# The last mixture-of-experts layer: 32 steps of 256 rows of one expert and four steps of 128-row tiles of any expert, in place of 39 steps of 256 rows

## The reference, cut to what matters

```python
def _L1_ffn_ref(x, Wr, br, W1, b1, W2, b2):
    K = 2
    E = Wr.shape[-1]                                   # 8 experts, W1 256 x 1024, W2 1024 x 256
    scores = jnp.einsum('bsd,de->bse', x, Wr) + br
    _, topk_idx = jax.lax.top_k(scores, K)
    indicator = jax.nn.one_hot(topk_idx, E, dtype=scores.dtype).sum(-2)
    weights = jax.nn.softmax(jnp.where(indicator > 0, scores, -jnp.inf), axis=-1)
    out = jnp.zeros_like(x)
    for i in range(E):
        xi = x * indicator[..., i:i + 1]
        h = jax.nn.relu(jnp.einsum('bsd,dh->bsh', xi, W1[i]) + b1[i])
        yi = jnp.einsum('bsh,hd->bsd', h, W2[i]) + b2[i]
        out = out + yi * weights[..., i:i + 1]
    return out
...
x = x + _L1_ffn_ref(_layernorm(x), L1_ffn_Wr, L1_ffn_br, L1_ffn_W1, L1_ffn_b1, L1_ffn_W2, L1_ffn_b2)
```

## Time and profile before

| | us |
|---|---|
| median of 3 runs | 1501.83 (1501.78 to 1501.98) |
| span of the profiled execution, first to last instruction | 1499.1 |
| of it `experts`, from the first row load (1050.4) to the end | 448.7 |
| PE busy over the span | 1272.8 (85%) |
| DVE / ACT / POOL busy over the span | 1052.8 / 821.5 / 523.5 |

### The profile page before, as it was taken

The page is one execution under the profiler, slowest core; times in us unless marked ns, Lnnn a source line. Parts: engine busy times, 40 slices in busy tenths (PEclk is TensorE's granted clock), DMA queues, the critical chain, the costliest instruction groups (busy, mean ns, idle before and its releaser), DMA issues. The chain is left out here.

```text
span 1499.1 us, 29224 instructions
## 1 busy us (share of the span) xinstructions
PE 1272.8 (85%) x8841; PEld 970.2 (65%) x8842; DVE 1052.8 (70%) x2033; ACT 821.5 (55%) x1209; POOL 523.5 (35%) x429
## 2 busy tenths in 40 slices
PE   8789999959975748998899998651899999999996
PEld 4456766744432647865567667650789989899995
DVE  5769999785699784557688887775456565656653
ACT  4565655465699677426778776650344343434431
POOL 2066676500000000000767675476023333332333
PEclk9899999979998558959999999555899999999998
DMA  6100000000134753001132232465222222222220
GB/s 216 60 8 1 0 0 0 1 1 0 43 147 163 262 205 122 1 1 45 31 123 75 87 123 70 142 211 178 69 47 51 42 49 46 42 46 44 50 40 10
DMA packets 63789, 106.87 MB, mean 71 GB/s; under 512 B 9776, under 2 KB 50832, under 8 KB 63088
## 3 DMA queue, kind: packets, MB, share of 16 engines
q1 hardware_dynamic: 49424, 89.17, 18.0%
q0 software_dynamic: 14304, 16.93, 6.2%
HBM read 67.89 MB, written 40.01 MB: 72 GB/s over the span
## 5 line engine op out<-in xcount | busy, mean ns | idle before, releaser
L2120 POOL DMA_INDIRECT out<-ex_yo,ex_mt x78 | 134.2, 1721 | 317.3 <-DVE ex_yo L2095 181.1
L2039 ACT ACTIVATE ex_hT<-ex_ps_h,e_b1T,e_unscale 128x256 f32<-128x256 f32 x312 | 150.8, 564 | 115.2 <-PE ex_ps_h L1997 115.2
L1997 PE MATMUL ex_ps_h<-ex_xT_hi,a_arena 128*128 128x256 f16 x1248 | 212.5, 274 | 0.0
L704 PE MATMUL at_ps_y<-c_VW,at_pT_hi 128*128 (+1 forms) x1024 | 172.8, 274 | 1.3 <-DVE main_x_res L835 1.3
L682 PE MATMUL at_ps_s<-a_arena,at_xnT_hi 128*128 (+1 forms) x512 | 158.6, 393 | 15.9 <-issue 13.1
L1997 PE MATMUL ex_ps_h<-ex_xT_lo,a_arena 128*128 128x256 f16 x624 | 171.0, 274 | 0.0
L2010 PE MATMUL ex_ps_y<-a_arena,ex_hT_lo 128*128 x624 | 170.1, 273 | 0.0
L2010 PE MATMUL ex_ps_y<-e_w_lo,ex_hT_hi 128*128 x624 | 170.1, 273 | 0.0
L2010 PE MATMUL ex_ps_y<-a_arena,ex_hT_hi 128*128 x624 | 170.1, 273 | 0.0
L959 POOL TENSOR_TENSOR at_sc<-at_sc,at_ri 128x960 f32<-128x960 f32 (+1 forms) x96 | 131.9, 1389 | 86.0 <-DVE at_ri L830 85.6
L1201 PE MATMUL gm_bank<-f_xq,f_wide 128*128 (+1 forms) x576 | 128.3, 383 | 20.7 <-ACT gm_stg L1239 16.2
(11 more groups left out here) (323 smaller groups left out, 2805.3 us busy)
## 6 DMA issues: line engine op xcount, KB each, us to landing
at_half<-in_L_ffn_W SPq DMA_DIRECT2D x32, 512.0 KB, 3.9
up_scratch<-gm_stg SPq DMA_DIRECT2D x16, 768.0 KB, 3.2
gm_stg<-up_scratch SPq DMA_DIRECT2D x16, 768.0 KB, 4.4
ex_row<-xs SPq DMA_DIRECT2D x39, 260.0 KB, 2.7
rt_stage<-in_L_ffn_W SPq DMA_DIRECT2D x16, 512.0 KB, 4.8
main_x_res<-in_x SPq DMA_DIRECT2D x8, 512.0 KB, 12.0
out<-main_x_res SPq DMA_DIRECT2D x8, 512.0 KB, 4.1
xs<-rt_pad SPq DMA_DIRECT2D x18, 130.0 KB, 2.1
```

Of the source, the lines that this page charges most:

```text
L704: last = nc.tensor.matmul(ps_y[:, 0:D], a[j][:, n, :], b[:, bass.ds(off + n * D, D)], start=(n == 0 and i == 0), stop=(n == NP - 1 and i = ...
L1997: last = nc.tensor.matmul(ps_h[:, n, :], a[:, bass.ds(e * WN + d * HID + n * P, P)], b[:, d, :], start=(m == 0), stop=(m == 3 * DT - 1))
L2039: last = nc.scalar.activation(hT[:, n, :], ps_h[:, n, :], ACT.Relu, bias=b1T[:, bass.ds(e * HT + n, 1)], scale=unscale[:, 0, bass.ds(e, 1)])
L2120: nc.gpsimd.indirect_dma_start(out=acc[:, :], out_offset=bass.IndirectOffsetOnAxis(ap=mt[j][:, q, 1:2].bitcast(U32), axis=0), in_=yo[j][:, ...
```

## The change

The steps become 36: 32 (`ND`) of 256 rows of one expert as before, and then four (`NM`) that take 128-row tiles, each tile of any expert, two to a step: seven tiles (`NH`), so three steps have two and the last has one. 32 groups of 256 and seven tiles of 128 are always enough for eight experts.

`table` has a place and an expert for 32 + 7 entries. Its computation on DVE shares out the steps of 256: first each expert's full groups of 256, then, while there are any to spare, experts with a rest of more than 128 rows, then those with a smaller rest; what is left becomes 128-row tiles. It has 31 DVE instructions behind the counts where there were 12. POOL sets two constants more (`CONSTS` 12).

In `experts`, every function asks `runs(i)` for the pieces of step i: one piece of 256 for i < 32, and one or two of 128 for the rest. For each piece of a mixed step SP looks up the place and issues a DMA; PE, ACT and DVE look up the expert's number once per piece; `up` and `relu` do each output tile once per piece, on 128 columns; `down` takes each half's expert; `weigh` and `keep_meta` have one instruction per piece where they use the expert's number. `rows_of` and `columns_of` cut the last step's work to its one tile. The loop now covers steps 4 to 27, and 28 to 35 are straight code.

```diff
-NTL = (2 * T + E * (TR - 1)) // TR
+ND = 2 * T // TR
+NH = 7
+NM = -(-NH // 2)
+NTL = ND + NM
...
-        CONSTS = 10
+        CONSTS = 12
...
-            g.iota(tid[:, :], pattern=[[1, NTL]], base=0, channel_multiplier=0,
+            g.iota(tid[:, 0:ND], pattern=[[1, ND]], base=0, channel_multiplier=0,
                    allow_small_or_imprecise_dtypes=True).then_inc(cst, 1)
+            g.iota(tid[:, ND:ND + NH], pattern=[[1, NH]], base=0, channel_multiplier=0,
+                   allow_small_or_imprecise_dtypes=True).then_inc(cst, 1)
+            g.memset(whole[:, E:E + 1], 0.0).then_inc(cst, 1)
...
+        def mixed(i):
+            return isinstance(i, int) and i >= ND
+
+        def runs(i):
+            if not mixed(i):
+                return [(i, 0, Q)]
+            return [(ND + 2 * (i - ND) + q, q, q + 1) for q in range(min(Q, NH - 2 * (i - ND)))]
...
-            for k in range(-lead, 4 + odd):
+            for k in range(-lead, 4):
                 step(k, k % 2)
-            with eng.Fori(2, NTL // 2 - 2, 1) as i:
+            with eng.Fori(2, (ND - 4) // 2, 1) as i:
                 for j in range(2):
-                    step(2 * i + (j + odd), (j + odd) % 2)
-            for k in range(NTL - 4, NTL + lag):
+                    step(2 * i + j, j)
+            for k in range(ND - 4, NTL + lag):
                 step(k, k % 2)
...
             def up(i, j):
-                e = look_up(nc.tensor, 1, i, E - 1)
+                spans = [(look_up(nc.tensor, 1, n, E - 1), slice(q0 * P, q1 * P)) for n, q0, q1 in runs(i)]
...
                     for n in range(4 * g, 4 * g + 4):
-                        m = 0
-                        for d in range(DT):
-                            for a, b in ((whi, xT_hi[j]), (whi, xT_lo[j]), (wlo, xT_hi[j])):
-                                last = nc.tensor.matmul(ps_h[:, n, :], a[:, bass.ds(e * WN + d * HID + n * P, P)], b[:, d, :],
-                                                        start=(m == 0), stop=(m == 3 * DT - 1))
-                                m += 1
+                        for e, at in spans:
+                            m = 0
+                            for d in range(DT):
+                                for a, b in ((whi, xT_hi[j]), (whi, xT_lo[j]), (wlo, xT_hi[j])):
+                                    last = nc.tensor.matmul(ps_h[:, n, at], a[:, bass.ds(e * WN + d * HID + n * P, P)], b[:, d, at],
+                                                            start=(m == 0), stop=(m == 3 * DT - 1))
+                                    m += 1
...
             def down(i, j):
-                e = look_up(nc.tensor, 1, i, E - 1)
+                spans = [(look_up(nc.tensor, 1, n, E - 1), range(q0, q1)) for n, q0, q1 in runs(i)]
...
-                for q in range(Q):
+                for e, q in ((e, q) for e, qs in spans for q in qs):
...
-                    for n in range(4 * g, 4 * g + 4):
-                        last = nc.scalar.activation(hT[:, n, :], ps_h[:, n, :], ACT.Relu,
+                    for n, (e, at) in ((n, span) for n in range(4 * g, 4 * g + 4) for span in spans):
+                        last = nc.scalar.activation(hT[:, n, at], ps_h[:, n, at], ACT.Relu,
                                                     bias=b1T[:, bass.ds(e * HT + n, 1)], scale=unscale[:, 0, bass.ds(e, 1)])
...
-                for q in range(Q):
+                for q in range(rows_of(i).stop):
                     need(pool, added, 16 * (Q * i + q))
                     pool.sem_inc(begun, 1)
...
-            pool.wait_ge(added, 16 * Q * NTL)
+            pool.wait_ge(added, 16 * (Q * ND + NH))
```

More of the change, by code:

```diff
@@ L1611, in route @@
         pad = s.sb("pad", [P, ROW])
[L1612 to L1616, removed]
+        ntf, nti, jump = s.sb("ntf", [P, 2, E]), s.sb("nti", [P, 2, E], I32), s.sb("jump", [P, 2, E])
+        cum, want, give, left = (s.sb(n, [P, 2, E]) for n in ("cum", "want", "give", "left"))
+        whole, lone, spare, twice = s.sb("whole", [P, E + 1]), s.sb("lone", [P, E]), s.sb("spare", [P, 1]), s.sb("twice", [P, 1])
+        tid = s.sb("tid", [P, ND + NH])
+        ge = s.sb("ge", [P, ND + NH, E])
+        tf = s.sb("tf", [P, 2, ND + NH])
         cnt = s.sb("cnt", [P, E], I32)
@@ L1902, in _ @@
             dve.sem_inc(cnt_r, 1)
[L1903 to L1909, removed]
@@ new lines, in _ @@
+            then(v.scalar_tensor_tensor(out=give[:, :, :], in0=cum[:, :, :], scalar=spare[:, 0:1], in1=want[:, :, :],
+                                        op0=ALU.is_le, op1=ALU.mult))
+            v.tensor_tensor(left[:, :, :], want[:, :, :], give[:, :, :], ALU.subtract)
+            then(v.tensor_tensor(lone[:, :], give[:, 0, :], give[:, 1, :], ALU.add))
+            v.tensor_tensor(whole[:, 0:E], ntf[:, 0, :], lone[:, :], ALU.add)
+            then(v.scalar_tensor_tensor(out=left[:, 0, :], in0=left[:, 0, :], scalar=2.0, in1=left[:, 1, :],
+                                        op0=ALU.mult, op1=ALU.add))
@@ new lines, in _ @@
+            v.tensor_tensor_scan(cum[:, 0, :], ones[:, 0:E], whole[:, 0:E], 0.0, ALU.mult, ALU.add)
+            v.tensor_scalar(jump[:, 0, :], whole[:, 0:E], -1.0, float(CAP // TR), ALU.mult, ALU.add)
+            v.tensor_tensor(lone[:, :], whole[:, 1:E + 1], whole[:, 0:E], ALU.subtract)
+            v.tensor_scalar(twice[:, :], whole[:, 0:1], 2.0, None, ALU.mult)
+            then(v.tensor_tensor_scan(cum[:, 1, :], ones[:, 0:E], left[:, 0, :], 0.0, ALU.mult, ALU.add))
+            v.scalar_tensor_tensor(out=jump[:, 1, :], in0=lone[:, :], scalar=2.0, in1=left[:, 0, :],
+                                   op0=ALU.mult, op1=ALU.subtract)
@@ new lines, in _ @@
+            for k, at in enumerate((slice(0, ND), slice(ND, ND + NH))):
+                last = v.tensor_tensor(ge[:, at, :], tid[:, at].unsqueeze(2).to_broadcast([P, (ND, NH)[k], E]),
+                                       per_tile(cum[:, k, :], k), ALU.is_ge)
+            then(last)
+            v.tensor_reduce(tf[:, 1, :], ge[:, :, :], AX.X, ALU.add)
+            then(v.tensor_scalar(jump[:, 1, :], jump[:, 1, :], float(CAP // P), None, ALU.add))
+            for k, at in enumerate((slice(0, ND), slice(ND, ND + NH))):
+                last = v.tensor_tensor(ge[:, at, :], ge[:, at, :], per_tile(jump[:, k, :], k), ALU.mult)
@@ L1917, in _ @@
+            v.tensor_scalar(table[:, 0, ND:ND + NH], tf[:, 0, ND:ND + NH], twice[:, 0:1], float(E * CAP // P), ALU.add, ALU.min)
             lows(highs_to(NK - 1), highs_to(NK))
@@ L1961, in load @@
             def load(i, j):
-                r = look_up(nc.sync, 0, i, E * CAP // TR)
+                rows = TR if not mixed(i) else P
                 need(sp, t_r, i - 1)
                 need(sp, meta_r, i - 1)
-                sp.dma_start(row[j][:, :, :], xs[bass.ds(r * TR, TR), :].rearrange("(q p) d -> p q d", p=P)
-                             ).then_inc(row_in[j], 16)
+                for n, q0, q1 in runs(i):
+                    r = look_up(nc.sync, 0, n, E * CAP // rows)
+                    sp.dma_start(row[j][:, q0:q1, :], xs[bass.ds(r * rows, rows), :].rearrange("(q p) d -> p q d", p=P)
+                                 ).then_inc(row_in[j], 16)
             def step(k, j):
```

83 lines of the change are left out of this document (56 added, 27 removed).

## The result

The changed kernel's median is 1480.45 us where the kernel before has 1501.8, a ratio of 0.9869 with a 95% interval of 0.9824 to 0.9914: faster by 21.3 us, and 1.5 us above the forecast of 1479. The execution that left the profile took 1477.83 us with a span of 1476.0; that of the kernel before took 1500.83 with 1499.1. So the two profiled executions are 23.0 us apart, where the sum had 22.8.

What follows compares the result with a forecast made beforehand. PE was taken to bound `experts`, its sequencer's addresses the mixed `up`. PE's 19.8 plus tail 3.3 less constants 0.3 gave 22.8 us saved: 1501.8 - 22.8 = 1479.0 us, range 1474 to 1485, at chance 0.70.

Steps and rivals of the forecast that it cites:

- mixed `up` of 32, 33, 34, 35: PE's `up` in the four mixed steps, paced by the sequencer's addresses: 7.95, 7.95, 8.6 and 4.1, sum 28.6 us.
- bare look-ups: Sequencer look-ups before the `down` of steps 31 to 34 leave PE idle: 0.9 once, 1.55 three times, 5.55 us.
- PE's balance: On PE, 71.2 us of removed work less the added `down`, transposes, mixed `up` and look-ups: 19.8 us saved.
- tail: After the last `down` but one, three additions on POOL instead of four: 16.6 against 19.95, 3.3 us saved.
- The pace of addresses: PE's sequencer in a mixed `up`: one address per 0.13 us, so 64 need 8.3 us and end last.
- B: Rival: the sequencer isn't the limit; a mixed `up` takes 5.2 us, nothing is bare, time 1463; chance 0.05.
- The lead: PE's sequencer runs 1.1 us ahead before `up`; a second look-up takes 0.65, leaving 0.45 us.
- Rival A: Weight loads pace small matmuls at 0.109 us; a mixed `up` takes 10.5, look-ups are hidden, time 1481.5; chance 0.14.
- Rival C: Clock falls for moments at bare look-ups: 1.7 us each, one to three of them, 1481 to 1484; chance 0.08.
- D: Rival: clock stays at 0.50 through all mixed steps; four `down` cost 21 us more, time 1507; chance 0.03.
- What was to be hidden: Per mixed step of about 15 us, ACT's at most 9.0 and DVE's 9 to 10 stay covered by PE.
- The table: In `route`, 19 more DVE instructions, 5.5 us, stay covered before the first row load; up to 5.5 if not.

Runs made afterwards that it cites:

- early2: The changed kernel with PE looking up all seven tiles' experts behind the `up` of steps 29 to 31, for mixed `up` and `down`; 1470.90 us.
- static_up: The changed kernel with fixed experts 0 and 1 in the mixed `up`, so PE computes no addresses there (output wrong); 1465.83 us.
- full36: The kernel before with 36 full steps instead of 39, the last three steps' rows left out of the computation; 1470.84 us.

## Why the prediction held, step by step

The forecast was the right case of the five: the sequencer's address computations set the pace of the mixed `up`, and its look-ups lie bare in front of the mixed `down`. By the profile of the changed kernel:

| term | predicted | found |
|---|---|---|
| mixed `up` of 32, 33, 34, 35 | 7.95, 7.95, 8.6, 4.1 | 7.95, 7.99, 8.78, 3.89 |
| bare look-ups | 0.9, 1.55, 1.55, 1.55 | 0.80, 1.46, 1.45, 1.51 |
| three mixed `down` | 15.7 | 15.84 |
| PE's balance | 19.8 | 19.96 |
| tail | 3.3 | 3.16 |
| constants on POOL | -0.3 | not to be told apart |
| saved in all | 22.8 | 23.0 to 23.1 |

- **The pace of addresses** carried over from a full `up` to a mixed one: most stand 0.124 apart, in the mean 0.130 to 0.132 over all 64. That the 20 addresses in the earlier trace rows were not held back by PE was the argument against B, and the mixed `up` of the changed kernel and of early2 bear it out: there PE is the one that waits, and the addresses come no faster. static_up has B's pace, 0.0558, but only because the addresses are gone.
- **The lead** of 1.1 us, of which a second look-up leaves 0.45, gave `up` 32 to the hundredth, which is partly luck: the lead was 0.53 (first address at 1402.87, first matmul at 1403.40), and from the last address to the end of the stage it took 0.18 instead of 0.1. early2 shows the worth of a lead directly, 7.95 against 7.0 us.
- **Rival A** fell by static_up, 0.0558 per pair of load and matmul. What the earlier trace rows say of f32 loads holds for these too: a load's duration isn't its pace.
- **Rival C** was priced from the right row but not whole. It happens, in two of five profiles, once and not up to three times, and costs 0.8 to 1.0 us, since here an engine that is paced by its sequencer gets part of a delay back. D didn't occur; by its own rows it was priced too high, since 48 x (0.20 - 0.106) is 4.5 us for a `down`, and three of them stand on the path, so 14 and not 21.
- **The tail** came out by two errors that cancel. I took 3.48 between additions as the cost of one; the earlier trace rows shows empty ones. In the changed kernel the first of the three carries rows of real tokens and the next is issued 4.27 behind it, 0.8 more than predicted, while from the last one to the end are 6.48 us instead of 7.06, a difference that no run explains. Nothing in the rows shown told full from empty additions; the DMA view of the same stretch would have. How many of the last additions are empty goes by the counts of the input, so the 3.16 hold for this one.
- **What was to be hidden** was: DVE has about 6.5 us of work in a mixed step, not 9 to 10, and ACT 6.4, between the half and the whole of 9.0.
- **The table** of `route` had its cover: from the counts to the weight splitting DVE took 6.2 us instead of 3.7 (2.5 more, not the 5.5 estimated), and the first row load kept its distance. DVE's timeline after, for the earlier trace rows:

```profile
1031.53 0.16 DVE L1908 CAST rt_cnt<-rt_run 128x8 int32<-128x8 f32 x1
...
1037.73 3.69 DVE L1830 SCALAR_TENSOR_TENSOR e_w_lo<-rt_stage,rt_wsc,a_arena 128x1024 f16<-128x1024 f32 x3
```

- **The remaining 1.5 us** between forecast and median are not in these terms. The sum is of one execution, and I subtracted it from a median. The 2.7 us that I called the time outside the span were 1.7 (1500.83 - 1499.1); the other 1.0 was the difference of that execution to the median, so I had treated a difference between executions as a constant. The changed kernel's executions spread over more, and its median lies 2.6 us above its profile. So the 22.8 came out to a few tenths between two single executions, which is partly luck; by the medians the saving is 21.3 us in the first set of runs and 19.1 in the second.

## What to carry to other kernels

Halving a tile doubles the instructions that a sequencer issues for the same work: before cutting a step into pieces whose addresses are known only at run time, count the computed addresses per us of PE's work, and compare them with their distance in the trace. Read look-ups once and early, at a place where the sequencer is ahead (9 us here, for seven tiles), since behind a stage that the sequencer paces each of its instructions is bare. And when a wait names an engine, see in that engine's timeline whether the instruction named is one that the waiting one reads.

## What the runs showed of the hardware

- Pairs of weight load (128 x 128) and matmul of 128 f16 columns run 0.0558 us apart when nothing on the sequencer holds them (static_up), though each load's row says 98 ns and each matmul's 219.
- An address computed on PE's sequencer has a row of 46 ns and comes every 124 ns. The Trainium skill (Perfetto Trace Analysis, Sequencer-only Instruction (DRAIN, etc)) says that the profile shows only the execution of a sequencer's instruction, not its fetch and decode. The 46 of 124 ns are consistent with that; no run here shows what fills the rest.
- An indirect addition of 128 rows of 1 KB, each behind the one before, takes 4.5 us from issue to issue (full36); one whose rows are all dropped 3.5, although it moves nothing (the kernel before).
- A short stop of PE of some 1.5 us among full work was followed by 3.4 us at a granted clock of 0.50 in two of five executions of the same program, and by none in the others.
